# Gated linear attention, rewritten: queries and keys decayed in place by a tree of totals, half sequences in turn, projections between the levels, the end by chunks

## The reference

```python
def _gla_scan(q, k, v, g):
    def step(S, inp):
        qt, kt, vt, gt = inp
        S = jnp.exp(gt)[..., None] * S + kt[..., None] * vt[..., None, :]
        ot = jnp.einsum('bhd,bhde->bhe', qt, S)
        return (S, ot)
...
u = x @ W_in.T
v, q, lg = jnp.split(u, 3, axis=-1)
q = jax.nn.silu(q); f = jax.nn.sigmoid(lg); k = 1.0 - f; g = jax.nn.log_sigmoid(lg)
o = _gla_scan(...)                      # one head of 128, over all 2048 tokens
o = o * jax.nn.sigmoid(x @ W_g1.T @ W_g2.T)
o = (o - mu) * jax.lax.rsqrt(var + LN_EPS) * ln_w
return o @ W_out.T
```

## Time and profile before

| | |
|---|---|
| time, median of 3 runs | 1712.25 us (1707.85 to 1714.1) |
| the profiled execution | 1715.76 us, span 1714.0 us |
| busy over the whole span | PE 1534.5 us (90%), DVE 1409.3 us (82%), ACT 922.9 us (54%), POOL 317.6 us (19%) |
| mean granted TensorE clock | 0.946 of full speed |
| this stage | from 1495.8 to 1599.2 us of the span |

### The profile page before, as it was taken

The page is one execution under the profiler, slowest core; times in us unless marked ns, Lnnn a source line. Parts: engine busy times, 40 slices in busy tenths (PEclk is TensorE's granted clock), DMA queues, the critical chain, the costliest instruction groups (busy, mean ns, idle before and its releaser), DMA issues. The chain is left out here.

```text
span 1714.0 us, 24094 instructions
## 1 busy us (share of the span) xinstructions
PE 1534.5 (90%) x8528; PEld 768.0 (45%) x8528; DVE 1409.3 (82%) x2448; ACT 922.9 (54%) x1748; POOL 317.6 (19%) x366
## 2 busy tenths in 40 slices
PE   6899999999999999699998888867999769986698
PEld 3111111111111111178883333324888658776587
DVE  6999999999999994476665999997767468789786
ACT  3188888888888888532235666653323323221232
POOL 3200000000000000000015878872000100133000
PEclk7599999999999999889998999999999979999699
DMA  3340100000000000200001222120000012100123
GB/s 102 114 135 26 33 29 26 23 23 23 23 23 23 23 25 11 49 1 1 1 1 56 69 67 70 62 74 1 1 1 1 1 50 92 60 1 1 50 71 105
DMA packets 41233, 66.36 MB, mean 39 GB/s; under 512 B 11422, under 2 KB 18383, under 8 KB 40392
## 3 DMA queue, kind: packets, MB, share of 16 engines
q1 hardware_dynamic: 41112, 64.82, 12.2%
HBM read 57.02 MB, written 6.88 MB: 37 GB/s over the span
## 5 line engine op out<-in xcount | busy, mean ns | idle before, releaser
L884 DVE TENSOR_REDUCE row_max<-ps 128x1 f32<-128x1024 f32 x512 | 601.0, 1219 | 34.6 <-PE ps L689 18.4
L807 ACT ACTIVATE probs<-ps 128x512 f32<-128x512 f32 x1024 | 529.1, 603 | 127.7 <-PE ps L704 127.4
L704 PE MATMUL ps<-q_stack,k_stack 51*128 51x512 bf16 x1024 | 346.6, 387 | 8.8 <-ACT probs L807 6.7
L689 PE MATMUL ps<-k_stack,q_stack 48*128 48x512 bf16 x1024 | 325.7, 403 | 20.2 <-DVE row_max L884 10.6
L721 PE MATMUL ps<-probs,v_head 128*16 128x512 f32 x2048 | 270.2, 600 | 0.0
L689 PEld LDWEIGHTS ps<-k_stack,q_stack 48*128 48x128 bf16 x1024 | 58.6, 96 | 368.4 <-DVE row_max L884 341.9
L1397 PE MATMUL ps<-s_hc,ident 128*128 128x512 f32 x256 | 137.8, 624 | 49.8 <-DVE s_hc L1670 44.7
L1050 ACT ACTIVATE x_gate<-ps 128x512 f32<-128x512 f32 x128 | 76.5, 599 | 184.1 <-PE ps L221 184.0
L1322 POOL TENSOR_TENSOR s_dbx<-s_dx,s_b_rows 128x512 f32<-128x512 f32 x128 | 159.4, 1270 | 35.6 <-DVE s_h L1661 35.0
L1661 DVE TENSOR_TENSOR_SCAN s_h<-ps,s_state,s_dbx 128x512 f32<-128x512 f32 x128 | 156.7, 1264 | 4.6 <-POOL s_dbx L1322 2.8
L704 PEld LDWEIGHTS ps<-q_stack,k_stack 51*128 51x128 bf16 x1024 | 76.0, 93 | 132.1 <-ACT probs L807 128.5
(11 more groups left out here) (343 smaller groups left out, 1924.9 us busy)
## 6 DMA issues: line engine op xcount, KB each, us to landing
s_b_rows<-s_b_dram SPq DMA_DIRECT2D x64, 256.0 KB, 3.1
y_spread<-y_probs_dram SPq DMA_DIRECT2D x128, 128.0 KB, 2.9
q_stack<-q_parts_dram SPq DMA_DIRECT2D x30, 96.0 KB
k_stack<-k_parts_dram SPq DMA_DIRECT2D x30, 96.0 KB
w_w<-w_dram SPq DMA_DIRECT2D x1, 2048.0 KB, 7.9
o_dram<-o_sb SPq DMA_DIRECT2D x64, 32.0 KB
q_stack<-q_parts_dram SPq DMA_DIRECT2D x30, 64.0 KB
k_stack<-k_parts_dram SPq DMA_DIRECT2D x30, 64.0 KB
```

The lines of the kernel that those rows point to most:

```text
L689: last = nc.tensor.matmul(core.ps[:, 2 * b + r, :], qst[buf][0:KROWS, u * P:(u + 1) * P], kst[buf][0:KROWS, key:key + CH], start=True, sto ...
L704: nc.tensor.matmul(core.ps[:, S_BANK + n % S_RING, :], kst[buf][HALF:ROWS, kt * P:(kt + 1) * P], qst[buf][HALF:ROWS, c * CH:(c + 1) * CH], ...
L807: nc.scalar.activation(probs[:, us % RING, c * CH:(c + 1) * CH], core.ps[:, S_BANK + n % S_RING, :], ACT.Exp).then_inc(exp_done, 1)
L884: nc.vector.tensor_reduce(mx[:, u, b:b + 1], core.ps[:, 2 * b:2 * b + 2, :], mybir.AxisListType.XY, ALU.max).then_inc(max_done, 1)
```

## The change

The stage is written anew; the class `LayerNorm`, which nothing else uses, is gone, so that later lines have other numbers.

- **Tree of totals.** GpSimd makes `spans[n]`, the product of the factors of each block of 2^n tokens, as seven products of neighbours, each half as long as the one before (1024, 512, ... 16 columns). `pre` and `suf`, their widening, and GpSimd's share of `qd` are gone.
- **In place.** `qd` and `kd` are decayed where they stand. A step multiplies the right halves of `qd` by the total of the left half beside them and the left halves of `kd` by that of the right half. After level 7 both are decayed over the whole tile.
- **Half sequences.** A level is two steps of 8 tiles; the 14 steps (level, half) go in turn.
- **Right halves only.** TensorE multiplies with the 64 query columns in right halves, and 8 tiles fill one bank. VectorE copies through a mask for levels 1 to 5, 512 columns a step. For levels 6 and 7 ScalarE copies the corner blocks with no mask (`take_corner`).
- **Projections.** After `lg` and `q`, the twelve chunks of `g1`, `v` and `gate` and a small product `mix` stand one by one behind the first 13 steps.
- **End by chunks.** Gate and statistics go by chunk, with roots on GpSimd as a power of -0.5. The gated rows are transposed unnormalized; centring and gain are folded into the output weight (`mixed`), and the scale of a row is applied when the product is added to `x_res`.

```diff
-            for step in range(NSTEP):
...
-                    for k in range(TPC):
-                        t = g * TPC + k
-                        last = nc.tensor.matmul(core.ps[:, 4 * (step % 2) + g, k * P:(k + 1) * P], tile_of(kk, t),
-                                                tile_of(qq, t), start=True, stop=True)
-                    last.then_inc(level_done, 1)
...
+            def multiply(level, s):
+                half = 1 << (level - 1)
+                pe.wait_ge(q_grown, HALVES * (level - 1) + s + 1)
+                if level > 1:
+                    pe.wait_ge(k_grown, HALVES * (level - 2) + s + 1)
+                if level == LEVELS:
+                    pe.wait_ge(level_taken, NC_ + HALVES * MASKED)
+                else:
+                    pe.wait_ge(level_taken, taken_before(level, s))
+                for k in range(HT):
+                    t = s * HT + k
+                    out = core.ps[:, level_bank(level, s), k * (P // 2):(k + 1) * (P // 2)]
+                    last = nc.tensor.matmul(out.rearrange("p (n h) -> p n h", h=half), tile_of(kd, t),
+                                            tile_of(qd, t).rearrange("p (n i h) -> p n i h", i=2, h=half)[:, :, 1, :],
+                                            start=True, stop=True)
+                last.then_inc(level_done, 1)
...
+            for i, (level, s) in enumerate(STEPS):
+                multiply(level, s)
+                if EARLY + i < len(ITEMS):
+                    project(EARLY + i)
...
+            for level, s in STEPS:
+                half = 1 << (level - 1)
+                dve.wait_ge(level_done, NC_ + HALVES * (level - 1) + s + 1)
+                dve.wait_ge(q_grown, HALVES * (level - 1) + s + 1)
...
+                right = sides(qd, level, s)[:, :, 1, :]
+                nc.vector.tensor_tensor(right, right, span_of(level, s, 0), ALU.mult).then_inc(q_grown, 1)
+                left = sides(kd, level, s)[:, :, 0, :]
+                nc.vector.tensor_tensor(left, left, span_of(level, s, 1), ALU.mult).then_inc(k_grown, 1)
+                if level <= MASKED:
...
+            for n in range(1, LEVELS + 1):
+                if n > 1:
+                    pool.wait_ge(span_made, n - 1)
+                pairs = spans[n - 1].rearrange("p (n i) -> p n i", i=2)
+                nc.gpsimd.tensor_tensor(spans[n], pairs[:, :, 0], pairs[:, :, 1], ALU.mult).then_inc(span_made, 1)
...
+            turn_k(0)
+            turn_k(1)
+            update(0)
+            update(1)
+            turn_k(2)
+            turn_k(3)
...
+            read(0)
+            update(2)
+            turn_o(0)
+            read(1)
+            project_out(0)
+            update(3)
+            turn_o(1)
+            read(2)
+            project_out(1)
+            turn_o(2)
+            read(3)
+            project_out(2)
+            turn_o(3)
+            project_out(3)
```

More of the change, by code:

```diff
@@ L2258, in gated_linear_attention @@
     nc, w = core.nc, core.w
+    HALVES, HT = 2, NT // 2
+    HCOLS = T // HALVES
+    MASKED = LEVELS - 2
+    RING, RING_BANK = 4, 4
+    ITEMS = [(name, c) for name in ("lg", "q", "g1", "v", "gate") for c in range(NC_)] + [("mix", 0)]
+    EARLY = 2 * NC_
+    NUMBER = {item: n for n, item in enumerate(ITEMS)}
+    STEPS = [(level, s) for level in range(1, LEVELS + 1) for s in range(HALVES)]
     with ExitStack() as ctx:
@@ L2263, in gated_linear_attention @@
         xnT = core.xnT
[L2264 to L2270, removed]
+        q_raw = sb("q_raw", [P, T])
+        qd = sb("qd", [P, T])
+        kd = sb("kd", [P, T])
+        f = sb("f", [P, T])
+        spans = [f[:]] + [sb(f"span{n}", [P, T >> n])[:] for n in range(1, LEVELS + 1)]
         v = sb("v", [P, NT, P])
@@ new lines, in project_out @@
+            def project_out(g):
+                pe.wait_ge(o_copied, g + 1)
+                if g >= 2:
+                    pe.wait_ge(added, g - 1)
+                for k in range(TPC):
+                    last = nc.tensor.matmul(core.ps[:, 2 + g % 2, k * P:(k + 1) * P], tile_of(o_T, g * TPC + k),
+                                            mixed[:], start=True, stop=True)
+                last.then_inc(out_done, 1)
+            for n in range(NC_):
+                if n == NC_ - 1:
+                    ln.turn(pe, NC_ - 1)
+                project(n)
@@ new lines, in take_corner @@
+            def take_corner(level, s):
+                half = 1 << (level - 1)
+                act.wait_ge(level_done, NC_ + HALVES * (level - 1) + s + 1)
+                act.wait_ge(level_taken, NC_ + HALVES * (MASKED - 1) + s + 1)
+                src = core.ps[:, level_bank(level, s), :].rearrange("p (t c) -> p t c", c=P // 2)
+                for b in range(P // (2 * half)):
+                    first = 2 * half * b
+                    nc.scalar.copy(att[first:first + half, s * HT:(s + 1) * HT, first + half:first + 2 * half],
+                                   src[first:first + half, :, b * half:(b + 1) * half]).then_inc(corner_taken, 1)
@@ new lines, in _ @@
+            for n in range(NC_):
+                if n == NC_ - 1:
+                    ln.copy_turned(act, NC_ - 1)
+                use(n)
+            for n in range(NC_, EARLY):
+                use(n)
+            nc.scalar.activation(gained[:], w["W_out"][:], ACT.Identity, scale=w["ln_w"][:]).then_inc(gain_done, 1)
+            for i, (level, s) in enumerate(STEPS):
+                if level > MASKED:
+                    take_corner(level, s)
+                if EARLY + i < len(ITEMS):
+                    use(EARLY + i)
@@ L2435, in _ @@
+            for g in range(NC_):
+                copy_k(g)
+            for g in range(NC_):
+                copy_o(g)
         @block.vector
```

386 lines of the change are left out of this document (215 added, 171 removed).

## The result

The kernel takes 1685.05 us after the change (median of 4 runs, 1682.77 to 1685.73) against 1712.61 before it (4 runs, 1707.85 to 1714.1): a ratio of 0.9841, 95% interval 0.982 to 0.9863. The forecast was 1685. The profiled execution took 1684.64 us, with a span of 1682.9.

The account below looks back on a forecast made before the run. VectorE was taken to bound the levels, busy 49.23 of 49.4 us. Terms 7.75 + 36.8 + 24.1 + 1.0 = 69.65 us against 97.0, 27.3 less, gave 1685 from the median 1712.25; 8-in-10 range 1670 to 1694.

Parts of the forecast that it names:

- Start of the levels: From ScalarE's last factor chunk at 1502.2 until TensorE starts level 1 at about 1509.95: 7.75 us.
- The 14 steps: Level steps, paced by TensorE, with twelve projection chunks and `mix` between them: 36.8 us.
- the term for the level products: TensorE's 16 records in each level step, at 0.116 us a record: 14 x 1.86 us.
- that for the chunks: Projections on TensorE between the level steps: 4 x 0.86 + 8 x 0.89 + 0.23 us for `mix`.
- the bound passes to TensorE: In the levels, TensorE needs 2.74 us a step with its projection, against VectorE's 1.83.
- The rival by which narrow products are shorter: Levels: 64 columns cost half of 128, VectorE stays the bound, 23.0 us instead of 36.8; time 1671, chance 0.12.
- VectorE idle some 0.9 us at each step: Sign expected in the profile after: in each level step VectorE waits some 0.9 us for TensorE.
- The tail: From TensorE's last level product to the next norm's rows, VectorE working without a gap after the first output: 24.1 us.
- 1.0 for the clock: Allowance in the tail for transposes and `read` running at 1.2 GHz behind a TensorE wait: 1.0, from 0 to 2.2 us.
- The rival with 1.2 GHz throughout the tail: Tail: TensorE at 1.2 GHz throughout, +4 us before the first output, later reads some 4 late; time 1693, chance 0.13.
- The clock in the levels: TensorE's granted clock would be 1.00 over the levels, as there are no pauses between the new steps.
- slower than before: Levels with TensorE at 1.2 GHz: 68.4 us instead of 36.8, time 1723 with the tail's 6 more; chance 0.03.

Follow-up runs that it names:

- the widths above: Changed kernel with level products of 128 or 32 query columns, or with 64 weight columns in level 7: 1686.98, 1686.22 and 1683.71 us.
- the filled kernel: Changed kernel with next norm's root earlier, 64 weight columns in level 7, one projection chunk ahead of the levels, five unused products at the stage's end: 1684.33 us.
- the tail's turns: Changed kernel with all states first, then all gates, then all sums, and TensorE's reads and updates ahead of the first transposed gate: 1690.57 us.
- GpSimd out of VectorE's way: Kernel before the change, with the decay of the queries moved from GpSimd to VectorE in steps 3 to 7: 1707.34 us, ratio 0.9969.

## Why the prediction was right, step by step

*Start of the levels*: 7.75 forecast, 7.38 measured (1498.12 to 1505.50). VectorE's first product beside GpSimd's tree was held as forecast (2.10 us, 1.22 alone). The second, beside the smaller products of the tree, was not (1.22 us), and that is most of the 0.4.

```profile
1498.99 1.89 POOL L2251 TENSOR_TENSOR g_span<-g_f 128x1024 f32<-128x1024 f32 x1 [4.85 <-DVE g_f L2475]
...
1499.86 2.10 DVE L2488 TENSOR_TENSOR g_qd<-g_q_raw,g_f 128x1024 f32<-128x1024 f32 x1 [0.95 <-ACT g_q_raw L2422]
```

*The 14 steps*: 36.8 forecast, 35.83 measured. I had put a record of 64 columns at 0.116 us, the middle of two neighbours (0.1115 for 128 columns, 0.121 for 16). By the starts of the groups, 1.73 us apart from what follows, it is 0.108, which lies outside both. The 14 groups took 24.3 us (26.0 forecast), the twelve chunks and `mix` 11.5 (10.8 forecast). So the term for the level products was 1.7 too large, that for the chunks 0.7 too small. With 32, 64 and 128 query columns a step of levels 1 and 2 with its chunk was 2.64 us each time.

That the bound passes to TensorE was the deciding step, and the widths above show its reason: the weights. The rival by which narrow products are shorter falls with it. The spacing by free dimension, which the Trainium skill gives ("TensorE: Matmul & The Clock Gate", "Back-to-back issue gap"), is in that section the one of isolated products; of pairs of a load and a product it says that both operations set the spacing. The traces agree with the second and not with the first: 32 to 128 columns made a difference of 0.08 us in 16 records.

Missed there, and hidden by TensorE: copies of 1.29 us in levels 1 and 2. With a quicker TensorE they would be on the path. The sign "VectorE idle some 0.9 us at each step" did not hold in these levels for that reason.

*The tail*: 24.1 and 1.0 for the clock forecast, 25.8 measured (1541.33 to 1567.13). The first state came 2.5 us in (2.45 forecast), the first gate 5.84 (5.9). The 1.0 for the clock was not paid: it was granted at 0.99. The rival with 1.2 GHz throughout the tail falls too. But this is in part luck. In two other traces with the same tail up to that point the clock did fall behind the pause for the third gate, to 0.66 (the filled kernel at 1556 to 1561, the one with projections ahead and 128 columns at 1563 to 1568), and cost 1.6 and 1.1 us, within the 0 to 2.2 that I had allowed. A term was missing: 2.10 us for the root of the next norm, behind another root on GpSimd's queue. I had written that roots "are gone" and had not put GpSimd's queue in order of time. The two errors, 1.0 too much and 2.1 too little, partly cancel; the rest of the tail took 0.4 less than the 24.1.

*The clock in the levels*: the forecast (1.00) was right and its reason was not. I argued that between the new steps there are no pauses. The kernel with projections ahead had none either from 1528 on, and stood at 0.50. What holds the clock in the changed kernel is what stands between the level products: projections of 512 columns in the first four steps and of 128 columns (eight records each) from then on. Moving them among the levels is worth 17.6 us. Of these, 14.5 are the clock, since they come back with level products of 128 columns and projections ahead; the other 3.1 are what the overlap hides, close to the 3 to 4 that I had expected of it. The mechanism of the rival "slower than before" is real: with the projections ahead, 10 of the 27.6 us were left. It did not come in because of where the projections stand, which I had chosen to hide their time and not for the clock.

*Not in the sum*: the next stage starts with TensorE at 0.50 after a rest of 5.05 us (before, 2.76 us of rest and 0.60 over its first 10.8 us). It costs 1.0 more, and 0.7 of it has come by VectorE's first `y_scores`, with four transposes that take 1.09 us instead of 0.63. The filler was to show whether the rest is the cause, and left it open.

```profile
1567.10:1578.00 10.90, 5.73 (x18) 4.25 (x18) 6.17 (x33) 4.46 (x10) 0.00 (x0) 0.50 0.00 0
```

The sum, 69.65 against 69.0, was nearer than its terms: measured less forecast is -0.4 at the start, -1.0 in the steps, +0.7 in the tail. That the time came within 0.1 us of 1685 is luck, then: with an unseen wait of 2.1 us and a term 1.7 too large, an error of 2 us would have been no surprise.

What was undone gives shares of the gain of 27.6 us, not to be added: projections among the levels 17.6, the tail's turns 5.5. GpSimd out of VectorE's way was worth 5.4 in the kernel before. What the full-length products, the shorter start and the missing norm operations gave is not taken apart.

## What to carry to other kernels

For small float32 products that each load their own weights, count weight columns, not query columns: cutting the moving side in half helps the engine that reads the result and left TensorE's step at 2.64 us. Where a change makes TensorE the bound with products of 64 columns, put wider ones between them (with 512 and 128 columns the clock was 1.00 here, with none 0.50) and read the granted clock of the stretch, since a busy share of 100% doesn't say at which level. And write the queue of every in-order engine in order of time, the nearly idle one too: the only wait of VectorE that the forecast lacked stood behind one instruction of 1 us on GpSimd, and moving one line took it away.

## What the runs showed of the hardware that I had not expected

- TensorE's clock stayed at 0.50 (1.2 GHz) from 1529.0 to 1558.8, 29.8 us of float32 products without a pause, 64 columns each. With 128 columns it was 1.00, pauses included (11.39 of 12.00 us busy), and with 64 columns and projections of 512 or 128 columns between the groups it was 1.00 too (35.80 us).
- A masked copy into a destination in runs of one or two values takes 1.29 us, side by side 0.73. A product with the same pattern takes 0.69, as in the other levels.
- Float32 products with 128 weight columns take the same time for 32, 64 and 128 moving columns (1.87, 1.90, 1.95 us for 16 records); with 64 weight columns 1.15 (their weight loads 1.01 instead of 1.87).
